# Products on the weights in the place of absent expert groups, at the front of a windowed-attention and mixture-of-experts kernel

## The reference

```
x = conv_block(x)       # LN, 7x7 shifted windows, 8 heads, softmax attention with relative bias and mask,
                        # projection, residual, LN, fc1 (64->256), gelu, LN, fc2 (256->64), residual
t = t + linear_attn(LN(t))   # k, v normalised per head of 4; kv = k^T v summed over all 3136 tokens of an image;
                             # gelu(proj(q kv + t)) + t
t = t + moe(LN(t))      # 8 experts, 64 -> 256 -> 64 with gelu; the top 2 by softmax of the logits, weighted
```

## Time and profile before

| | |
|---|---|
| median of 3 runs | 8270.77 us (8262.04 to 8276.08) |
| the profiled execution: time, span | 8265.89 us, 8264.0 us |
| granted clock of TensorE over the span | 0.996 |
| busy, of the span | PE 95%, DVE 76%, ACT 75%, POOL 57% |
| instructions | 254328, of these 77810 matmuls of PE |

### The profile page before, as it was taken

How to read it: one execution, slowest core, us unless ns; L and a number is a source line. 1 busy time by engine, 2 the same in 40 slices (tenths; PEclk the granted TensorE clock), 3 DMA queues, 4 the chain that set the end, 5 groups by cost and what they waited for, 6 DMA issues and landing times. The chain is left out here.

```text
span 8264.0 us, 254328 instructions
## 1 busy us (share of the span) xinstructions
PE 7871.5 (95%) x77810; PEld 5168.3 (63%) x77810; DVE 6299.5 (76%) x26070; ACT 6214.3 (75%) x10999; POOL 4684.1 (57%) x7940
## 2 busy tenths in 40 slices
PE   6899999999999999999999999999999999999997
PEld 5666666666666666666666666666666666666663
DVE  4477778777777877877777787787777778777773
ACT  2377777777777777777777777777777777777774
POOL 1355556566565565655556555565555565565553
PEclk9999999999999999999999999999999999999999
DMA  0001111111111111111111111111111111111111
GB/s 24 4 26 36 36 35 34 37 36 33 37 36 32 36 37 33 35 37 36 33 36 37 32 36 37 33 36 37 36 33 37 34 34 37 37 32 36 36 34 42
DMA packets 216033, 281.61 MB, mean 34 GB/s; under 512 B 30371, under 2 KB 214216, under 8 KB 214344
## 3 DMA queue, kind: packets, MB, share of 16 engines
q1 hardware_dynamic: 214600, 264.20, 11.3%
HBM read 235.04 MB, written 28.90 MB: 32 GB/s over the span
## 5 line engine op out<-in xcount | busy, mean ns | idle before, releaser
L1281 ACT ACTIVATE ht<-ps,be 128x392 f32<-128x392 f32 x4096 | 2253.6, 584 | 346.0 <-PE ps L707 170.6
L707 PE MATMUL ps<-ht,we 128*64 128x392 f32 x8192 | 1584.4, 508 | 39.4 <-ACT ht L1281 25.0
L697 PE MATMUL ps<-xs,we_hi 128*128 128x392 f16 x4096 | 1370.6, 335 | 166.9 <-ACT ht L1281 166.8
L697 PE MATMUL ps<-xs,we_lo 128*128 128x392 f16 x4096 | 1349.2, 329 | 0.0
L1088 POOL TENSOR_TENSOR sc<-sc,mx 113x392 f32<-113x392 f32 x1024 | 896.0, 884 | 707.4 <-DVE mx L872 707.2
L707 PEld LDWEIGHTS ps<-ht,we 128*64 128x64 f32 x8192 | 498.9, 136 | 714.0 <-issue 550.8
L1174 ACT ACTIVATE pt<-ps 98x392 f32<-98x392 f32 x1024 | 506.9, 495 | 512.3 <-PE ps L557 487.1
L697 PEld LDWEIGHTS ps<-xs,we_hi 128*128 128x128 f16 x4096 | 410.2, 100 | 685.0 <-issue 384.6
L1074 POOL TENSOR_TENSOR rs<-ve,cs 98x4 f32<-98x4 f32 x768 | 781.2, 1017 | 21.4
L1105 POOL TENSOR_TENSOR kvsd<-kvsd,cs 98x128 f32<-98x128 f32 x256 | 101.9, 398 | 1218.0 <-ACT kvsd L1247 1218.0
L1067 POOL TENSOR_TENSOR ve<-mv,cs 98x4 f32<-98x4 f32 x768 | 154.2, 201 | 981.8 <-DVE mv L830 981.7
(11 more groups left out here) (185 smaller groups left out, 18858.7 us busy)
## 6 DMA issues: line engine op xcount, KB each, us to landing
gb<-gates SPq DMA_DIRECT2D x1024, 196.0 KB, 3.7
xg<-in_x SPq DMA_DIRECT2D x256, 98.0 KB
out_y<-yo SPq DMA_DIRECT2D x256, 98.0 KB
gates<-gtt SPq DMA_DIRECT2D x256, 12.2 KB
bias<-in_rel SPq DMA_DIRECT2D x1, 1200.5 KB
bias<-in_w SPq DMA_DIRECT2D x2, 512.0 KB
gb<-in_amask SPq DMA_DIRECT2D x2, 300.1 KB
we<-in_w SPq DMA_DIRECT2D x1, 512.0 KB
```

Source lines behind the costliest of these rows:

```text
L697: last = pe.matmul(pH[b % 2][:, 0:GTOK], we1[half][:, 128 * b:128 * (b + 1)], xs[:, g.j % 2, :], start=(half == 0), stop=(half == 1))
L707: last = pe.matmul(pY[C * e:C * (e + 1), 0:GTOK], we2[:, b, :], ht[:, b % 8, :], start=(h == 0), stop=(h == 1), skip_group_check=True)
L1281: act.activation(ht[:, b % 8, :], pH[b % 2][:, 0:GTOK], ACT.Gelu, bias=be1[:, b:b + 1], scale=1.0 / WSCALE).then_inc(S["h_ready"], 1)
```

## The change

Where an iteration's step in{b} has no group yet (n + a < 0), PE now issues two f16 products: the 128 weights of block b, high and low half, on the first 392 columns of the same half of `we1`, into pH0 or pH1 as the real step would. Nobody reads the result, and the first real product of a bank starts its sum anew. They have no wait and signal nothing. `early` is given for PE alone.

```diff
--- before.py
+++ after.py
@@ -342,13 +342,15 @@
         LEAD = max(a for plan in PLAN.values() for _, a in plan)
         LAG = -min(a for plan in PLAN.values() for _, a in plan)
 
-        def program(eng, plan, steps):
+        def program(eng, plan, steps, early={}):
 
 
             def iteration(at, n, c, like):
                 for name, a in plan:
                     if exists(name, like + a):
                         steps[name](Group(at, n, c, a, like))
+                    elif like + a < 0 and name in early:
+                        early[name]()
 
             bodies = TOTAL // BODY
             head = min(2, bodies)
@@ -698,6 +700,11 @@
                                      start=(half == 0), stop=(half == 1))
                 last.then_inc(S["e1_psum"], 1)
 
+            def warm(b):
+
+                for half in range(2):
+                    pe.matmul(pH[b % 2][:, 0:GTOK], we1[half][:, 128 * b:128 * (b + 1)], we1[half][:, 0:GTOK], start=True, stop=True)
+
             def expert_out(g, p):
                 bank_free(pe, f"out{p}", g)
                 now(pe, "h_ready", g, 0, 4 * p + 3)
@@ -730,7 +737,7 @@
                 steps[f"out{p}"] = lambda g, p=p: expert_out(g, p)
             for part in range(4):
                 steps[f"mixp{part}"] = lambda g, part=part: mix(g, part)
-            program(pe, PLAN["pe"], steps)
+            program(pe, PLAN["pe"], steps, {f"in{b}": lambda b=b: warm(b) for b in range(BLOCKS)})
 
 
         @block.vector
```

## The result

The changed kernel took 8253.72 us (median of 13 runs, 8239.75 to 8269.75) against 8272.18 us of the kernel before in the same rounds (13 runs, 8262.04 to 8277.77). The ratio is 0.9978, 95% interval 0.9970 to 0.9986: 18 us faster. The forecast was 8268 with a range of 8222 to 8293, that is, 2 us faster than the 8270.8 known then.

A forecast was written before the change was run, and what follows sets the result against it. PE bounds the kernel, busy 95% of the span, its front at 1.2 GHz. Nine iterations -8, n = -1 0, n = 9 -1, start +7.3: about -2 us from 8270.8, rounded to 8268; range 8222 to 8293.

The forecast's parts named there:

- The start: Before the first transpose of z: a burst of 28 pairs ends 7.3 us later than z, on the path.
- An iteration all high: One front iteration with pairs, wholly at the higher clock level: 28.0 us, against 35.4 before.
- rival 1: Clock holds from the first burst through the front: -68 us, 8203; chance 0.28 for held wholly or with one fall.
- The clock oscillates: Main case, front iterations: clock falls in two holes and returns behind pairs; 34.5 us each, 0.9 less; chance 0.56.
- G: Segment from the end of fc10 to the next pT0, 5.5 us; PE waits for the exponential, clock expected to fall.
- C: Segment from the end of kv to proj, 3.7 us; PE waits for ot, clock expected to fall.
- nearly every one to pay: Both holes expected to lower the clock in nearly every front iteration; 34.5 us taken per iteration.
- The ends of the front: n = -1, expected to change by 0, and n = 9 up to the present rise, expected at -1 us.
- Behind it nothing changes: After the first expert pair at 450.8, which moves by the whole difference, the steady loop was to stay as before.
- Rival 2: Pairs mostly run low in the front, each costing 0.65 us: +69 to +76 us, about 8342; chance 0.10.
- half-way case of rival 1: Only one of the two falls happens per front iteration, 31 us each: -40 us, 8235; within the 0.28 chance.
- the case forecast as likeliest: Oscillating clock in the front as summed: net about -2 us, own range 8243 to 8292; chance 0.56.

The follow-up runs named there:

- e3: Changed kernel with the same 416 products and weight loads on 8 columns in place of 392; 8272.61 us, 1.0006 of the kernel before.
- e10: Kernel before with 128 small f16 products (256 PE instructions) added in the idle time of the setup; 8268.69 us, 0.9998 of the kernel before.
- e2: Changed kernel with 5 more pairs at in1 and 4 more at in7, iterations n = -1 to 8; 8217.40 us, 0.9935 of the kernel before.
- e6: Changed kernel with 5 more pairs at in1 alone (wait for the exponential), n = -1 to 8; 8218.02 us, 0.9938 of the kernel before.
- e7: Changed kernel with 4 more pairs at in7 alone (wait for ot), n = -1 to 8; 8241.42 us, 0.9967 of the kernel before.
- e5: Kernel before with 32 small f32 products (128 instructions) in PE's idle time of the setup; 8288.23 us, 1.0023 of the kernel before.
- e11: Changed kernel with 5 more pairs at in1, 4 at in7, and 128 more instructions in the setup; 8202.64 us, 0.9917 of the kernel before.
- e4: Changed kernel with only the pairs of n = -4 and -3, 32 in all; 8289.92 us, 1.0024 of the kernel before.
- e9: Changed kernel with 16 small f32 products (64 instructions) in PE's idle time of the setup; 8267.48 us, 0.9997 of the kernel before.

## Why the prediction was right, and where it was off

- *TensorE is at 1.2 GHz through the front, and f16 products on the whole array raise it.* Shown: e3, with the same instructions on 8 columns, is at 0.50 for 351.6 us and gains nothing. That only f16 work can raise it is not shown; e10 and e3 have one rise of 3.4 us over f32 work.
- *The start, +7.3 us.* 7.6 in the trace (89.83 against 82.23), with the rise after 12 products, as assumed. Of these 7.6 the steps up to the first pT0 give back 1 us (107.05 against 100.47).
- *An iteration all high, 28.0 us.* 28.1 in e2. A front held high was worth about what rival 1 said: the front of e2 ends 65 us before that of the kernel before, and rival 1 had 68.
- *The clock oscillates, with falls in G and C, back at in2 to in5.* Shown by the windows and by e2, e6 and e7. The rule of the Trainium skill (TensorE: Matmul & The Clock Gate, "Why this matters for your kernels") would have kept the clock up across waits of 2 us; this trace doesn't agree: it fell within the waits of 1.96 us or up to 2.1 us behind them, with f32 work following.
- *The size.* This was off: the whole difference was put at 2 us and measured at 18, and the forecast came in range because the range is 71 us wide. The term that was mis-sized is the one of nine iterations, from "nearly every one to pay", 34.5 us each. Its prices were good: an iteration with both falls took 34.8 to 37.9 us in the trace (34.7 forecast), one with a single fall 30.5 to 32.2 (31). What failed is how often: the fall in G comes in all nine, that in C in four. So they took 33.4 us on average (300.5 / 9). The base was off as well: 35.4 us was used for all nine, and with the longer n = 7 and 8 they took 36.0 before (324.3 / 9). Gained were 2.6 us each, not 0.9: 23.8 us in place of 8.
- *The ends of the front.* n = -1 gained 3.7 us (29.9 to 26.2 from pT0 to pT0) where 0 was expected. From the pT0 of n = 9 to the loop 1.2 us were lost (37.9 against 36.7) where 1 was to be gained. In all the front gave 19.7 us where about 2 were expected.
- *"Behind it nothing changes."* This was wrong. The loop took 7.8 us longer in this execution. It has no wait on issue between 500 and 7880, as the kernel before has none, but its clock is at 0.50 for 47.8 us against 30.7. At half the clock these 17.1 us more can cost up to 8.6 us (an estimate), which is enough for the 7.8. So in this execution falls of the clock can account for it, and waits on issue can't. Why there are more falls stays open: e5 and e11 show that the length of the loop depends on how many instructions stand ahead of it, but e3, with as many as the changed kernel, has 7494.1.
- Rival 2 (mostly low) did not come: the clock of the front is 0.80, 60% of it high. The half-way case of rival 1, one fall only, was put at 31 us per iteration: five of the nine are such iterations. Its sum has a slip: 8270.8 less the 40 us stated is 8231, and the 8235 given would go with 36 us.

So the case forecast as likeliest was the one that came, towards its faster edge: 8254 in its range of 8243 to 8292. The mechanism was right and the size was not: the front gave ten times what was summed.

## What to carry to other kernels

Work that only keeps the clock up should stand where the engine waits, for there it is free. Here it paid to cover the waits themselves: pairs spread over the iteration brought 0.2%, nine pairs more per iteration in the two waits, with a burst cut to what the idle time holds, brought 0.9%. Five pairs in the wait that lowers the clock every time brought three times what four in the other one did (36 and 12 us). Judge such a change by the duration of one and the same product in the trace, since the granted clock has no record before its first change. And before a difference of 0.2% is put down to an edit, move the code by some instructions without changing it: here that alone was worth 0.23%.

## What the runs showed of the hardware that was not expected

- The loop's length depends on how many instructions PE has ahead of it: 7512 to 7513 us with 128 added, 7507 with 896, 7509 with 1192; 7491 to 7500 with 0, 256, 704, 832, 992, 1032, 1104 and 1320. Modulo 256 the slow ones are 128, 128 and 168, the others 0, 0, 192, 64, 224, 8, 80 and 40. Three kernels were forecast by this rule before they ran and agreed in sign. The amounts tried fit a period of 512 or 1024 as well. That it is the place of the code which counts is the reading that fits, and not shown by itself; what the waits on issue at the start of a pass are made of was not tried either.
- The longer loops have more of the clock's records at 0.50: 51.2 to 68.3 us in e2, e4, e5 and e9, against 30.7 to 47.8 in the nine loops up to 7500 us.
- A clock that is up can fall around waits of 1.7 to 2.3 us when the work behind them is f32: with the 1.96 us before pT0 it did so in all nine iterations n = 0 to 8 of the changed kernel, with the 1.74 us before proj in four of them. It isn't held by the f32 products of this front (0.50 for 368.6 us in e4, with PE busy 310.16 of them).
